# A graph network on one core: the last layer's two stages, one after the other or as one

## The reference

```python
def reflection(a, b):
    h = relu(concatenate([a, b], axis=1) @ W1.T + b1)      # 32 -> 64 -> 16
    return h @ W2.T + b2
def householder(v):
    vn = v / maximum(norm(v, axis=1, keepdims=True), 1e-12)
    return eye(d)[None] - 2.0 * vn[:, :, None] * vn[:, None, :]
F_s, F_d = householder(reflection(xs, xd)), householder(reflection(xd, xs))
L_sd = -einsum('eki,ekj->eij', F_s, F_d)
coef = deg_inv_sqrt[src] * deg_inv_sqrt[dst]
msg_s = coef[:, None] * einsum('eij,ej->ei', L_sd, xd)
msg_d = coef[:, None] * einsum('eji,ej->ei', L_sd, xs)
out = x - zeros_like(x).at[src].add(msg_s) - zeros_like(x).at[dst].add(msg_d)
return relu(out)
```

## Time and profile before

| | us |
|---|---|
| median of 3 runs (lowest to highest) | 8023.22 (8023.16 to 8027.09) |
| the profiled execution | 8028.09 |
| its span, first to last instruction | 8026.3 |
| TensorE busy in the span | 5857.5 (73%) |
| VectorE busy | 5670.7 (71%) |
| GpSimd busy | 4181.5 (52%) |
| ScalarE busy | 1607.1 (20%) |
| mean granted clock of TensorE | 0.754 |

### The profile page before, as it was taken

One profiled execution on the slowest core, in us unless ns is written; L12 is line 12 of the kernel. 1 busy time (PEld: TensorE's weight loads), 2 busy tenths in 40 slices (PEclk: granted clock), 3 DMA queues, 4 the chain that ended last, 5 costly groups with the idle time before them and its releaser, 6 DMA issues. The chain is left out here.

```text
span 8026.3 us, 119080 instructions
## 1 busy us (share of the span) xinstructions
PE 5857.5 (73%) x33540; PEld 3931.1 (49%) x33541; DVE 5670.7 (71%) x10923; ACT 1607.1 (20%) x2670; POOL 4181.5 (52%) x4125
## 2 busy tenths in 40 slices
PE   4444442664446888877999995545899899999999
PEld 2433342554444555554555552544244466666555
DVE  5666662743336999989999999999000488888898
ACT  0111110011103555541222220441000122222000
POOL 0777774777775777775777770000000477776000
PEclk9555555555557999998999997798899655555999
DMA  3222223321122333351111110220576211111000
GB/s 112 71 67 69 69 69 80 85 50 37 38 43 56 84 85 85 84 76 40 41 41 41 41 41 22 93 102 33 220 284 263 63 33 33 31 33 29 0 0 1
DMA packets 492400, 550.24 MB, mean 69 GB/s; under 512 B 130191, under 2 KB 395399, under 8 KB 478712
## 3 DMA queue, kind: packets, MB, share of 16 engines
q1 hardware_dynamic: 349464, 483.93, 18.5%
q0 software_dynamic: 131584, 43.10, 5.8%
q10 hardware_dynamic: 11232, 21.73, 1.0%
HBM read 452.30 MB, written 96.00 MB: 68 GB/s over the span
## 5 line engine op out<-in xcount | busy, mean ns | idle before, releaser
L1307 POOL DMA_INDIRECT sh_ring<-node,sh_idx x832 | 826.0, 993 | 1594.8 <-DVE sh_idx L1997 1333.4
L1551 POOL DMA_INDIRECT slots<-rec,row x832 | 858.9, 1032 | 353.8 <-issue 274.3
L1307 POOL DMA_INDIRECT mx_ring<-node,mx_idx x832 | 856.1, 1029 | 319.9 <-issue 224.0
L938 POOL DMA_INDIRECT mid_ring<-typed,mid_idx x832 | 839.3, 1009 | 258.9 <-issue 253.3
L446 POOL DMA_INDIRECT slots<-rank_staged,rank_row_i x782 | 795.5, 1017 | 262.2 <-issue 246.8
L426 PE MATMUL rank_found<-rank_next_sb,rank_hot_hi_t 26*128 26x128 f32 x1568 | 367.5, 424 | 573.9 <-ACT rank_next_sb L408 568.5
L1657 PE MATMUL sm_sums<-sm_both,sm_hot 128*128 128x512 f32 x1664 | 784.4, 594 | 0.2 <-DVE sm_both L1578 0.2
L1147 PE MATMUL mid_sums<-mid_ring,mid_hot_d 128*128 128x17 f32 x1664 | 391.5, 375 | 419.9 <-DMA mid_ring<-typed,mid_idx 408.1
L426 PEld LDWEIGHTS rank_found<-rank_next_sb,rank_hot_hi_t 26*128 26x128 f32 x1568 | 341.4, 325 | 599.0 <-issue 591.8
L1147 PEld LDWEIGHTS mid_sums<-mid_ring,mid_hot_d 128*128 128x128 f32 x1664 | 383.4, 312 | 436.0 <-issue 436.0
L2158 PE MATMUL srl_sums<-srl_outer,srl_hot_lo 128*128 128x400 f32 x1664 | 560.5, 500 | 7.4 <-DVE srl_outer L2140 7.4
(11 more groups left out here) (406 smaller groups left out, 12100.0 us busy)
## 6 DMA issues: line engine op xcount, KB each, us to landing
strips<-near SPq DMA_DIRECT2D x100, 1562.5 KB, 8.7
mx_far<-far_row SPq DMA_DIRECT2D x208, 256.0 KB
rank_key_row<-key_rows SPq DMA_DIRECT2D x98, 512.0 KB
near<-adj_whole SPq DMA_DIRECT2D x175, 256.0 KB, 2.0
sm_low<-low_row SPq DMA_DIRECT2D x208, 128.0 KB
sh_low<-low_row SPq DMA_DIRECT2D x104, 256.0 KB, 3.3
feat_t<-mid_out ACTq DMA_DIRECT2D x104, 204.0 KB
mx_feat<-feat_t SPq DMA_DIRECT2D x208, 102.0 KB
```

The source lines that it names most:

```text
L938: pool.indirect_dma_start(ring[:, n % DEEP, j, 0:D], None, m.typed, bass.IndirectOffsetOnAxis(ap=idx[:, t:t + 1], axis=0)).then_inc(gather ...
L1307: pool.indirect_dma_start(ring[:, n % AHEAD, j, :], None, table, bass.IndirectOffsetOnAxis(ap=idx[:, t:t + 1], axis=0)).then_inc(gathered[ ...
L1551: pool.indirect_dma_start(m.slots2, bass.IndirectOffsetOnAxis(ap=row2[:, t:t + 1], axis=0), rec2[:, t, :], None).then_inc(m.ordered, 16)
```

## The change

`to_sources` is gone; its work is part of `sheaf_messages`, two batches behind on TensorE and one behind on VectorE.

- TensorE: `sources(n-2, ...)` runs in four groups of two tiles, between the other groups of turn n. `spread` is one fp32 matmul per tile in place of three bf16 ones.
- VectorE: one operation makes both one-hots of a batch in bf16 (`hots`); `spread_far(n-1)` makes `hot_hi`, now in PSUM, and the outer product while ScalarE takes the root of batch n; squares, the split in three parts and the copy of the near ends are gone from it.
- ScalarE: squares the vectors, casts all one-hots to fp32 (`hot`) and copies the near ends (`near_ends`); the copy into `m.parts` is gone.
- GpSimd waits for `coef_s` and `near_s` in place of `ends_s` before it reuses a ring slot.
- `hot_hi` shares a PSUM bank with `v_ps`, so `vectors` waits for `outer_s`.

The core of the diff:

```diff
-            gather(pool, m.node20, idx, ring, idx_s, gathered, ends_s, TB, total)
+            pool.wait_ge(idx_s, 1)
+            for n in range(total):
+                if n >= AHEAD:
+                    pool.wait_ge(coef_s, n - AHEAD + 1)
+                    pool.wait_ge(near_s, n - AHEAD + 1)
...
+            def hots(r):
+                n, h = r.n, r.mod(2)
+                wait(dve, cast_s, n - 1)
+                wide = [P, TB, P, 2]
+                now = lows[:, bass.ds(n, 1), :].rearrange("q o (a t) -> q (o a) t", t=2)
+                nc.vector.tensor_tensor(hot_16[:, h], now[:, :, None, :].to_broadcast(wide), iota[:, None, :, :].to_broadcast(wide),
                                         ALU.is_equal).then_inc(hot_s, 1)
...
+                dve.wait_ge(xd_s, n + 1)
+                nc.vector.tensor_copy(ends[:, h, :, 1, :], xd[:, :, 0:D]).then_inc(ends_s, 1)
                 dve.wait_ge(gathered[slot], (r.div(AHEAD) + 1) * 16 * TB)
+                wait(dve, both_s, n - 1)
+                nc.vector.tensor_tensor(coef[:, h, :], xd[:, :, D], ring[:, slot, :, D], ALU.mult).then_inc(coef_s, 1)
+
+            def spread_far(r):
+                n, h = r.n, r.mod(2)
+                now = bass.ds(n * TB, TB)
+                wait(dve, outer_s, n)
+                nc.vector.tensor_tensor(hot_hi, hi[:, now][:, :, None].to_broadcast([P, TB, NB]),
+                                        m.iota_row[:, None, 1:NB + 1].to_broadcast([P, TB, NB]), ALU.is_equal).then_inc(hi_s, 1)
+                wait(dve, far_used, n - 1)
+                dve.wait_ge(both_s, n + 1)
+                dve.wait_ge(hi_s, n + 1)
+                nc.vector.tensor_tensor(outer[:, h].rearrange("q t (s d) -> q t s d", d=D),
+                                        both[:, h, :, 0, :][:, :, None, :].to_broadcast([P, TB, NB, D]),
+                                        hot_hi[:, :, :, None].to_broadcast([P, TB, NB, D]), ALU.mult).then_inc(outer_s, 1)
...
+                hots(r)
                 dve.wait_ge(v_s, 2 * n + 2)
+                nc.vector.tensor_tensor(flat(vec), v_ps[:, :, :], m.mlp_b2[:, None, :].to_broadcast([P, TB, 2 * D]), ALU.add).then_inc(bias_s, 1)
                 if inside(n + 2, total):
                     far_hots(r.plus(2))
+                dve.wait_ge(sq_s, n + 1)
+                nc.vector.tensor_reduce(norm[:, :, :], sq[:, :, :, :], AX.X, ALU.add).then_inc(norm_s, 1)
+                if inside(n - 1, total):
+                    spread_far(r.plus(-1))
                 dve.wait_ge(root_s, n + 1)
...
-                link(nc.vector.tensor_copy(three[:, h, :, 0:D], near))
-                link(nc.vector.tensor_tensor(rest[:, :, :], near, three[:, h, :, 0:D], ALU.subtract))
-                link(nc.vector.tensor_copy(three[:, h, :, D:2 * D], rest[:, :, :]))
-                nc.vector.tensor_tensor(three[:, h, :, 2 * D:3 * D], rest[:, :, :], three[:, h, :, D:2 * D],
-                                        ALU.subtract).then_inc(three_s, 1)
...
+            def near_ends(r):
+                n, h, slot = r.n, r.mod(2), r.mod(AHEAD)
+                act.wait_ge(gathered[slot], (r.div(AHEAD) + 1) * 16 * TB)
+                nc.scalar.copy(ends[:, h, :, 0, :], ring[:, slot, :, 0:D]).then_inc(near_s, 1)
+
+            def turn(r):
+                n, h = r.n, r.mod(2)
+                act.wait_ge(bias_s, n + 1)
+                nc.scalar.activation(sq[:, :, :, :], vec[:, :, :, :], ACT.Square).then_inc(sq_s, 1)
                 act.wait_ge(norm_s, n + 1)
                 nc.scalar.activation(norm[:, :, :], norm[:, :, :], ACT.Sqrt).then_inc(root_s, 1)
                 if inside(n + 1, total):
                     network(n + 1)
-                act.wait_ge(three_s, n + 1)
-                nc.scalar.copy(m.parts[:, bass.ds(n * TB, TB), :], both[:, h, :, 0, :]).then_inc(kept_s, 1)
+                act.wait_ge(hot_s, n + 1)
+                wait(act, used, n - 1)
+                wait(act, far_used, n - 1)
+                nc.scalar.copy(hot[:, h], hot_16[:, h]).then_inc(cast_s, 1)
+                if inside(n + 2, total):
+                    act.wait_ge(swap_s, 2 * n + 2)
+                    near_ends(r.plus(2))
...
             def turned_ends(n, h):
+                pe.wait_ge(near_s, n + 1)
                 pe.wait_ge(ends_s, n + 1)
...
+                        last = nc.tensor.matmul(sums[:, bass.ds(b * D, D)], hot[:, h, k, :, j % 2], both[:, h, j, 1, :], start=False,
+                                                stop=True, skip_group_check=True)
...
+            def sources(n, h, first, end):
+                pe.wait_ge(outer_s, n + 1)
+                for j in range(first, end):
+                    last = nc.tensor.matmul(far_sums[:, 0:NB * D], hot[:, h, TB // 2 + j // 2, :, j % 2], outer[:, h, j, :], start=False,
+                                            stop=True, skip_group_check=True)
+                if end == TB:
+                    last.then_inc(far_used, 1)
+
             def turn(q, h):
                 n = 2 * q + h
                 if inside(n + 1, total):
                     turned_ends(n + 1, 1 - h)
+                if inside(n - 2, total):
+                    sources(n - 2, h, 0, 2)
                 if inside(n - 1, total):
                     spread(n - 1, 1 - h)
+                if inside(n - 2, total):
+                    sources(n - 2, h, 2, 4)
                 if inside(n + 1, total):
                     network(n + 1)
+                if inside(n - 2, total):
+                    sources(n - 2, h, 4, 6)
                 if inside(n + 2, total):
                     far_ends(q + 1, h)
                 if inside(n + 1, total):
-                    for half in range(2):
-                        vectors(n + 1, half)
+                    vectors(n + 1, 0)
+                if inside(n - 2, total):
+                    sources(n - 2, h, 6, TB)
+                if inside(n + 1, total):
+                    vectors(n + 1, 1)
```

More of the change, by code:

```diff
@@ L1905, in _ @@
         def _(pool):
-            gather(pool, m.node20, idx, ring, idx_s, gathered, ends_s, TB, total)
+            pool.wait_ge(idx_s, 1)
[3 more added lines that the diff above has]
+                    pool.wait_ge(near_s, n - AHEAD + 1)
+                for j in range(TB):
+                    t = n * TB + j
+                    pool.indirect_dma_start(ring[:, n % AHEAD, j, :], None, m.node20,
+                                            bass.IndirectOffsetOnAxis(ap=idx[:, t:t + 1], axis=0)).then_inc(gathered[n % AHEAD], 16)
         @block.sync
@@ L2022, in turn @@
                     network(n + 1)
-                act.wait_ge(three_s, n + 1)
-                nc.scalar.copy(m.parts[:, bass.ds(n * TB, TB), :], both[:, h, :, 0, :]).then_inc(kept_s, 1)
+                act.wait_ge(hot_s, n + 1)
[5 more added lines that the diff above has]
+                    near_ends(r.plus(2))
+            for k in range(2):
+                near_ends(Turn(0, k, AHEAD))
             network(0)
-            batches(act, total, 1, 1, turn)
+            rounds(act, total, AHEAD, AHEAD, turn)
         @block.tensor
@@ L2031, in _ @@
             clear(nc, m, sums[:, :])
+            clear(nc, m, far_sums[:, :])
             def far_ends(q, h):
@@ L2037, in far_ends @@
                 pe.wait_ge(hot_t_s, n + 1)
-                wait(pe, vec_s, n)
+                wait(pe, ends_s, n)
+                wait(pe, coef_s, n)
                 for k in range(TB // 2):
@@ L2062, in vectors @@
                 if half == 0:
-                    wait(pe, norm_s, n)
+                    wait(pe, bias_s, n)
+                    wait(pe, outer_s, n - 1)
                 for j in range(half * TB // 2, (half + 1) * TB // 2):
@@ L2075, in spread @@
                     for j in (2 * k, 2 * k + 1):
-                        for part in range(3):
-                            last = nc.tensor.matmul(sums[:, bass.ds(b * D, D)], hot[:, h, k, :, j % 2],
-                                                    three[:, h, j, part * D:(part + 1) * D], start=False, stop=True,
-                                                    skip_group_check=True)
+                        last = nc.tensor.matmul(sums[:, bass.ds(b * D, D)], hot[:, h, k, :, j % 2], both[:, h, j, 1, :], start=False,
+                                                stop=True, skip_group_check=True)
                 last.then_inc(used, 1)
+            def sources(n, h, first, end):
[5 more added lines that the diff above has]
+                    last.then_inc(far_used, 1)
             def turn(q, h):
@@ L2165, in finish @@
+            batches(pe, total, 3, 3, turn)
+            last = total - 1
+            sources(last - 1, 1 - last % 2, 0, TB)
+            spread(last, last % 2)
+            sources(last, last % 2, 0, TB)
 def finish(nc, m, out):
@@ L2295, in build @@
             rb = on(scope)
-            m.parts, m.wide3 = rb("parts", [P, NT, D]), rb("wide3", [P, NB, 3, HW], BF16)
+            m.wide3 = rb("wide3", [P, NB, 3, HW], BF16)
```

(1 more changed line is left out.)

127 lines of the change are left out of this document (38 added, 89 removed).

## The result

| | before | after |
|---|---|---|
| median of 4 runs, us | 8024.2 | 7933.1 |
| lowest to highest | 8023.2 to 8027.1 | 7920.4 to 7948.3 |
| profiled execution | 8028.1 | 7933.3 |
| mean granted clock of the whole run | 0.754 | 0.813 |

The ratio is 0.9886, 95% interval [0.9874, 0.9898]: **1.1% faster**, 91 us. The forecast was 8050 and slower; the range (7765 to 8255) holds the time.

The account below looks back on a forecast made before the run. TensorE at half clock was taken to bound the message stage (10.76 us a batch). At mean clock 0.80, P = 12.2/c + 1.2 = 16.45 and 6362 + 103 P = 8056, less 5: 8050 us, range 7765 to 8255.

Parts of the forecast that it names:

- The frame: Whole kernel: 6332 us to the first batch, 103 batches of P, then 23 and 8: T = 6362 + 103 P.
- TensorE's work: Merged batch on TensorE: sources 5.4, spread 1.7, network 1.86, vectors 1.71, turned ends 0.84, far ends 0.66; 12.2 us at full clock.
- rival D: Spread on TensorE: spaced fp32 weights load at half speed, +1.7 in P, 7960 or 8270 us; chance 0.05.
- ScalarE's queue: Near ends queued behind the 1.88 us cast on ScalarE make TensorE's turned ends stall 1.65 us a batch at full clock.
- VectorE I had too high: VectorE's busy time per merged batch: 9.54 before, less removed work, plus one-hots, hot_hi and outer product; 12.1 us.
- Rival C: ScalarE: squares and roots need different function tables, two loads of 1.28 a batch; 8090 to 8320 us; chance 0.05.
- c = 0.80: Mean TensorE clock of the merged stage, between adjacency-stage 0.67 and 0.98; P = 12.2/c + 1.2 gives 16.45.
- wrong sign: Whole kernel forecast at 8050 us, slower; break-even at c = 0.815; chances faster 0.45, same 0.07, slower 0.48.
- The place: Clock falls between the fourth source group and the next: 0.85 vectors, 1.65 stall, 0.84 turned ends, 3.3 us.
- a mixed clock over 0.82: Merged stage: clock falls in part of the batches but its mean exceeds 0.82, so faster; chance 0.20 of mixed clock's 0.58.
- Rival A: Merged stage: full clock throughout, P 13.65 to 13.9, 7765 to 7790 us; chance 0.24.
- B, half clock in most batches: Merged stage: source groups of two tiles too short to bring the clock back; 8881 us; chance 0.08.

Follow-up runs that it names:

- near_first_quick: Changed kernel with the near ends' copy ahead of the cast of the one-hots on ScalarE; 7664.95 us, 0.9545 of the kernel before.
- twice_cast_quick: Changed kernel with ScalarE casting the one-hots twice, one after the other, ahead of the near ends; 8629.9 us, 1.0751 of the kernel before.
- fill_stall_quick: Changed kernel with two added products of zeros on TensorE in its wait ahead of the turned ends; 7839.2 us, 0.9763 of the kernel before.
- sources_whole_quick: Changed kernel with all eight source tiles in one group behind the turned ends, not two at a time; 8086.5 us, 1.0071 of the kernel before.
- dense_before: Kernel before with eight added fp32 products of zeros per message-stage batch, two at each of four places; 8100.6 us, 1.0090 of the kernel before.
- three_parts: Changed kernel with near ends ahead of the cast, and the earlier spread (bf16 one-hots, message in three bf16 parts); 7645.5 us, 0.9521 of the kernel before.
- near_early: Changed kernel with near ends ahead of the cast on ScalarE and the fourth source pair ahead of the network; 7670.0 us, 0.9552 of the kernel before.
- no_sources: Changed kernel without its source matmuls, outer products still made; 7685.7 us, 0.9577 of the kernel before.

## Why the prediction was right or wrong

**The frame holds.** 6362 + 103 P was forecast; the profiled 7933.3 less 103 x 15.20 leaves 6367.3. The first batch starts at 6338.8 instead of 6331.7, 7.1 us that I had put at nothing and whose cause no run parts; the end is 2.6 shorter than the 31 that I had.

**TensorE's work was put 0.6 too small.** At full clock it is 14.36 - 1.54 = 12.8 instead of 12.2 (12.65 in near_first_quick, where no group drains into a wait). From the second batch of the timeline, start to start: sources 1.35 + 1.52 + 1.46 + 1.43 = 5.76 (5.4 forecast, which is 1.35 a group: three of the four take 0.08 to 0.17 more), spread 1.80 (1.7), network 1.91, turned ends 0.87, far ends 0.65, vectors 0.88 + 0.95. The bound of 3.4 for spaced fp32 weights, rival D, is refuted. Far ends are 0.61 to 0.66 at either level, as supposed.

**ScalarE's queue was right, and it was the most useful step.** Cast 1.90 (1.88), near ends 0.29 (0.30), TensorE's wait 1.54 (1.65), VectorE's wait for the squares 0.87 (0.8). near_first_quick removes TensorE's wait, twice_cast_quick doubles it. The price of 1.65 us at full clock was what fill_stall_quick and near_first_quick measure, 170 us in all. VectorE I had too high: busy 88.5% of 12.65 is 11.2, not 12.1. I had started from 10.76 less its one long wait, 9.54, where the row has it busy 81.11 of 100, which is 8.7 a batch; the additions of 2.5 were right. hot_hi takes 0.37 us in PSUM as it did in SBUF. Rival C is out, since the traces have no table load in the batches.

**The clock was the step that failed.** The step is the choice of c = 0.80, a clock too low for this mix of groups. With c = 0.80 the forecast's P = 12.2/c + 1.2 is 16.45. With the clock of the stage, 0.93, it is 14.3; with the work of 12.8 too, 15.0, against 15.20 measured. The work's error was unfavourable (with it c = 0.80 would have given 17.2), so the whole wrong sign is the clock's. The place was right: in 42 batches the clock falls behind the wait, in 22 of them within the turned ends and in 20 within the first source pair, and in 39 it is back before the second pair. The size was not: a mixed clock over 0.82 had a chance of 0.20 in the forecast. I took it from two stretches of the adjacency stage (0.67 and 0.98) by the share of dense passes, and set the source passes alone (5.4 of 13.9) against all matmuls of a stretch (48 of 100). That comparison was no guide: of the two stretches the one with more matmul time, 64.66, has the lower clock. The runs show that the share doesn't carry over either: sources_whole_quick and near_first_quick have the same passes and hardly any idle time, and 0.71 against 0.99. What differs is how the passes are spaced; and with the spacing of the changed kernel the length of the wait takes the clock from 0.99 (none) to 0.93 (1.54) and 0.69 (3.4, twice_cast_quick).

**Where the gain came from**, as a sum in us per batch, each step but one a run: 10.76 for the message stage before; + 0.70 for the source passes at the four places, which double the clock (dense_before, 11.46); + 1.19 for the fp32 spread, computed from 1.80 - 0.61, giving 12.65 as near_first_quick has; + 1.65 for the wait on ScalarE (14.31, fill_stall_quick); + 0.90 for the clock behind it (15.20). In exchange the source stage's 5.5 are gone. So the merge was worth 3.6 us a batch, some 360 us in all, and the order of two instructions gave back 2.55 of them. That the computed step closes the sum to the hundredth is in part luck: taken out again in three_parts, it gave 0.27, since VectorE then set the batch.

**The rivals.** Rival A (full clock, 7765 to 7790) did not come. It had the right sign, and 1.00 is nearer to the measured 0.93 than 0.80 is, but its time is further off (143 us or more, the forecast 117). fill_stall_quick has its clock and takes 7839, 50 over the 7789 of that case, which are the 0.46 us of P (14.31 for 13.85) that the work was short. Its condition, that the stretch between the last and the first source pair be short enough, has the right place but not the right measure: near_early has a stretch nearly as long as the changed kernel's, without idle time, and full clock. B, half clock in most batches, did not come, but what it said of the pairs did in part: in three batches of the changed kernel and in every second one of twice_cast_quick the clock stays low past several source pairs. The Trainium skill, page TensorE: Matmul & The Clock Gate, section Part 1: The HAM clock gate, says that activity releases the throttle. As I read it, the runs don't agree: TensorE is busy 99.9 to 100 of 100 us at 0.50 in no_sources, at 0.74 in sources_whole_quick and at 1.00 in dense_before. Which instructions fill the time makes the difference.

What stays open: why the changed kernel's clock falls in just four batches of ten, and stays down through three of them; no run here settles that. So the runs give what the clock costs in each arrangement, but no way to have worked out 0.93 beforehand.

## What to carry to other kernels

Before an in-order engine gets a long new instruction, look for a short one behind it that a third engine waits for; here a swap of two instructions, free of cost, was worth 3.4% of the kernel and three times the change itself. Where a stage is all light matmuls at half clock, try dense work in among them, in small groups between the others: here it was almost free, and in one lump (sources_whole_quick) the whole gain was gone. And where the clock falls in a part of the batches, take the idle time out first and judge the change then: with it the change was 1.1% faster on one chip and 0.6% slower on another, without it over 4% faster on both sorts.

## What the hardware showed that I had not expected

- Added work made a kernel faster: two products of zeros a batch, four passes, took 94 us off (fill_stall_quick), and eight in the kernel before, sixteen passes, cost 0.70 us a batch instead of 5.4 (dense_before).
- 1.9 us more of waiting in a batch cost 6.8 (twice_cast_quick), since a clock that has fallen can stay down for 24 us.
- Chips differ: the same program before takes 8024 to 8030 us on some and 10195 to 10217 on two others, and the changed kernel, run on one chip of each sort, is 1.1% faster and 0.6% slower. Neither of the two was used at another time, so whether it is the chip or its state at that time stays open.
- Squares, roots, relu and copies alternate on ScalarE in every batch without a table load.
- fp32 weights two elements apart load as fast as packed ones: in near_early the 16 passes of the spread take 1.79 us to the next start, and so do the 16 of the vectors.
